# Graph passes gather into a ring of sixteen tiles in place of four; the last pass scatters a block eight steps behind its gather from eight tiles

## What is computed

```python
def gcn_layer(x, src, dst, W, b, n_nodes):              # layer 0, twice
    h = x @ W
    norm = dis[src] * dis[dst]
    agg = segment_sum(h[src] * norm[:, None], dst, n_nodes)
    return agg + h * (dis * dis)[:, None] + b

def _gcn_conv(h, W, b, row, col, norm, num_nodes):      # layer 3, six times
    h = h @ W
    agg = segment_sum(h[row] * norm[:, None], col, num_nodes)
    return agg + b

x = _layernorm(x + layer0(x))     # two GCN convolutions
x = _layernorm(x + layer1(x))     # gated edges
x = _layernorm(x + layer2(x))     # graph attention
x = _layernorm(x + layer3(x))     # GCN widths 128-64-32-16-32-64-128, then h @ Wf + bf
return x
```

## Time and profile before

| what | us |
|---|---|
| three executions: median, lowest, highest | 11700.1, 11695.49, 11714.07 |
| span of the profiled execution, first to last instruction | 11674.7 |
| busy in the span: DVE, POOL, PE, ACT | 8085.7, 7388.3, 6602.9, 5916.2 |
| g1 (689.0 to 1479.9) and g2 (1479.9 to 2402) | 790.9 and 922.1 |
| layers 1 and 2 (2402 to 7066.5) | 4664.5 |
| g3, g4, g5, g6, g7 | 698.5, 608.2, 742.5, 640.3, 646.8 |
| g8 (10402.8 to the end) | 1271.9 |

### The profile page before, as it was taken

One profiled execution on the slowest core, in us unless ns is written; L12 is line 12 of the kernel. 1 busy time (PEld: TensorE's weight loads), 2 busy tenths in 40 slices (PEclk: granted clock), 3 DMA queues, 4 the chain that ended last, 5 costly groups with the idle time before them and its releaser, 6 DMA issues. The chain is left out here.

```text
span 11674.7 us, 142292 instructions
## 1 busy us (share of the span) xinstructions
PE 6602.9 (57%) x32436; PEld 5435.0 (47%) x32436; DVE 8085.7 (69%) x33889; ACT 5916.2 (51%) x13869; POOL 7388.3 (63%) x6801
## 2 busy tenths in 40 slices
PE   5036666656664666677566666753455565543343
PEld 3035655545554666677456565742233343322222
DVE  7357799946667999899888884445466666764444
ACT  0024467757677999899577773321133332322222
POOL 7734478867776888666376664556554555556665
PEclk8568888878886555688678875555577556655555
DMA  4977778832224777444244443433344333332221
GB/s 136 317 236 236 237 270 289 289 96 70 70 70 156 235 234 235 135 141 141 86 154 165 160 165 114 136 105 83 84 131 128 92 97 87 116 88 55 55 57 51
DMA packets 1019502, 1694.48 MB, mean 145 GB/s; under 512 B 304878, under 2 KB 535081, under 8 KB 1018595
## 3 DMA queue, kind: packets, MB, share of 16 engines
q1 hardware_dynamic: 782752, 1361.06, 34.9%
q0 software_dynamic: 175936, 218.82, 8.4%
q10 hardware_dynamic: 59970, 105.49, 2.7%
HBM read 988.03 MB, written 707.78 MB: 145 GB/s over the span
## 5 line engine op out<-in xcount | busy, mean ns | idle before, releaser
L1340 POOL DMA_INDIRECT g_got<-scaled,row_src x2352 | 2230.9, 948 | 1640.0 <-issue 684.0
L298 PE MATMUL g_a_p_z<-sb_L_gnn_W,g_a_u_t 128*128 128x128 f32 (+3 forms) x2574 | 650.8, 397 | 1045.8 <-ACT g_a_u_t L1185 374.3
L902 DVE SCALAR_TENSOR_TENSOR g_sums<-g_got,first,g_sums 128x128 f32<-128x128 f32 (+3 forms) x3136 | 866.0, 276 | 389.4 <-remote 113.4
L298 PEld LDWEIGHTS g_a_p_z<-sb_L_gnn_W,g_a_u_t 128*128 128x128 f32 (+1 forms) x2574 | 482.4, 265 | 1218.4 <-issue 584.0
L906 DVE SCALAR_TENSOR_TENSOR g_sums<-g_sums,cont,g_got 128x128 f32<-128x128 f32 (+3 forms) x3128 | 882.3, 282 | 110.0 <-DVE g_sums L902 74.6
L1185 ACT COPY g_a_u_t<-g_a_p_t 128x512 f32<-128x512 f32 (+3 forms) x495 | 225.3, 455 | 1357.5 <-remote 779.5
L298 PE MATMUL g_bb_p_z<-sb_L_gnn_W,g_bb_u_t 128*128 128x128 f32 (+2 forms) x4302 | 831.4, 361 | 116.5 <-DVE g_bb_z L1077 79.0
L298 PEld LDWEIGHTS g_bb_p_z<-sb_L_gnn_W,g_bb_u_t 128*128 128x128 f32 x4302 | 753.6, 261 | 165.7 <-issue 134.8
L1185 ACT COPY g_bb_u_t<-g_bb_p_t 128x1024 f32<-128x1024 f32 (+2 forms) x294 | 233.8, 795 | 1111.8 <-issue 541.4
L1340 POOL DMA_INDIRECT g_got<-xs,idx_src x392 | 370.8, 946 | 470.1 <-DVE g_a_own L1021 279.1
L1252 POOL DMA_INDIRECT out<-g_a_o,idx_out x396 | 395.4, 998 | 370.3 <-ACT g_a_o L350 254.7
(11 more groups left out here) (495 smaller groups left out, 24005.0 us busy)
## 6 DMA issues: line engine op xcount, KB each, us to landing
raw<-gb_u SPq DMA_DIRECT2D x98, 768.0 KB
xs<-f_o ACTq DMA_DIRECT2D x97, 516.0 KB
f_x<-in_x ACTq DMA_DIRECT2D x97, 512.0 KB
g_bb_own<-in_x SPq DMA_DIRECT2D x97, 512.0 KB
wide<-g_bb_o SPq DMA_DIRECT2D x97, 512.0 KB
g_bb_own<-wide SPq DMA_DIRECT2D x97, 512.0 KB
g_bb_res<-in_x SPq DMA_DIRECT2D x97, 512.0 KB
x<-g_bb_o SPq DMA_DIRECT2D x97, 512.0 KB
```

Source lines behind the costliest of these rows:

```text
L298: last = nc.tensor.matmul(dst_psum[0:p, q * g * width:(q * g + n) * width], turned_tile[0:n * k, q * P:q * P + p], weight[0:n * k, 0:n * w ...
L902: nc.vector.scalar_tensor_tensor(out=self.firsts, in0=new, scalar=first[:, col], in1=self.firsts, op0=ALU.mult, op1=ALU.add).then_inc(run_ ...
L1340: pool.indirect_dma_start(got[b.s4][:, c * row:(c + 1) * row], None, table, bass.IndirectOffsetOnAxis(ap=index[:, b.n * CH + c:b.n * CH + ...
```

## The change

The ring `got` has sixteen tiles, named by block number modulo 16. The gather of block n waits until block n - 16 is combined, and also until the gather of block n - 4 has landed; this second wait is needed because the four landing semaphores stay four. In g1, which also copies a column out of the gathered tile, the wait for that copy moves from n - 4 to n - 16 too. In g8 the output has eight tiles in place of four, the scatter is eight steps behind the gather in place of four, `normalise` waits for the landing of the scatter of block n - 8, and the scatter of block n waits for the landing of that of block n - 4. No arithmetic changes, and the number of DMAs on every engine stays.

```diff
+RING = 16
+OUT_RING = 8
...
-                dve, tile = nc.vector, self.tiles[b.s4 % len(self.tiles)]
+                dve, tile = nc.vector, self.tiles[b.n % len(self.tiles)]
...
-                    if b.after(UNROLL):
-                        nc.scalar.wait_ge(scattered[b.s4], past(scattered[b.s4]) + b.turn * CH * DMA)
+                    if b.after(OUT_RING):
+                        nc.scalar.wait_ge(scattered[b.s4], past(scattered[b.s4]) + (b.turn + 1 - OUT_RING // UNROLL) * CH * DMA)
...
                 nc.gpsimd.wait_ge(self.m_.finished, b.n + 1)
+                if b.after(UNROLL):
+                    nc.gpsimd.wait_ge(scattered[b.s4], past(scattered[b.s4]) + b.turn * CH * DMA)
...
-                        self.o_s[b.s4][:, c * D:(c + 1) * D], None, bounds_check=N - 1, oob_is_err=False
+                        self.o_s[b.n % OUT_RING][:, c * D:(c + 1) * D], None, bounds_check=N - 1, oob_is_err=False
...
-                got = [sb(f"got{s}", [P, CH * row]) for s in range(UNROLL)]
+                got = [sb(f"got{s}", [P, CH * row]) for s in range(RING)]
...
                             if b.after(UNROLL):
-                                pool.wait_ge(mark_a.combined, b.n - UNROLL + 1)
+                                pool.wait_ge(gathered[b.s4], past(gathered[b.s4]) + b.turn * CH * DMA)
+                            if b.after(RING):
+                                pool.wait_ge(mark_a.combined, b.n - RING + 1)
                                 if keep_rows:
-                                    pool.wait_ge(indexed, b.n - UNROLL + 1)
+                                    pool.wait_ge(indexed, b.n - RING + 1)
...
-                            pipeline(pool, [(gather, 0, NBE), (na.scatter, 4, NBA)])
+                            pipeline(pool, [(gather, 0, NBE), (na.scatter, 8, NBA)])
```

More of the change, by code:

```diff
@@ L946, in __init__ @@
                 self.own_s = [sb(f"{n}_own{s}", [P, G * k]) for s in range(2)]
-                self.o_s = [sb(f"{n}_o{s}", [P, G * m]) for s in range(UNROLL if scatters else 2)]
+                self.o_s = [sb(f"{n}_o{s}", [P, G * m]) for s in range(OUT_RING if scatters else 2)]
                 self.from_own = self.deep or self.after or (edges is None and not self.plain)
@@ L1335, in gather @@
                             if b.after(UNROLL):
-                                pool.wait_ge(mark_a.combined, b.n - UNROLL + 1)
+                                pool.wait_ge(gathered[b.s4], past(gathered[b.s4]) + b.turn * CH * DMA)
+                            if b.after(RING):
+                                pool.wait_ge(mark_a.combined, b.n - RING + 1)
                                 if keep_rows:
-                                    pool.wait_ge(indexed, b.n - UNROLL + 1)
+                                    pool.wait_ge(indexed, b.n - RING + 1)
                             for c in range(CH):
                                 pool.indirect_dma_start(
-                                    got[b.s4][:, c * row:(c + 1) * row], None, table,
+                                    got[b.n % RING][:, c * row:(c + 1) * row], None, table,
                                     bass.IndirectOffsetOnAxis(ap=index[:, b.n * CH + c:b.n * CH + c + 1], axis=0)
@@ L1376, in keep_row @@
                             dve.wait_ge(gathered[b.s4], gathers_before(gathered[b.s4], b))
-                            nc.vector.tensor_copy(at_window(row_src, b), got[b.s4][:, k:CH * row:row]
+                            nc.vector.tensor_copy(at_window(row_src, b), got[b.n % RING][:, k:CH * row:row]
                                                   ).then_inc(indexed, 1)
```

## The result

The changed kernel takes 11886.06 us (median of four, 11855.92 to 11898.55) against 11697.8 us before on the same chip: ratio 1.0158, 95% interval 1.0141 to 1.0174, 1.6% slower. 11830 was forecast, range 11620 to 11930. The profiled execution has a span of 11881.7 us and a time of 11883.46.

The account below looks back on a forecast made before the run. The consumer (DVE with PE and ACT), held during POOL's long indirect-DMA runs, sets the pace in most passes; DVE bounds g2. 11674.7 + 128 (six passes +118, g8 +10) + 25.4 gives 11828, said as 11830 us; range 11620 to 11930.

Parts of the forecast that it names:

- the sign of being right: Observation named in advance as confirming the forecast: among others, g3 to g7 each 8 to 30 us longer.
- 12 f: End of g1, g3 to g7: twelve more blocks left when POOL falls silent, each costing f, the busiest engine's 3.16 to 5.57 us.
- 91 - 18.2 T: Start of g1, g3 to g7: first run 91 us longer, sparing 18.2 steady-state blocks of T (6.01 to 7.94 us) each.
- the bound of +189: Upper bound for g1, g3 to g7 in sum, if nothing is combined while POOL issues; +118 us was taken.
- g8: Ring and later scatter in g8: extra steps +30 us, end -21, net taken as +10; bounds -243 and +45.
- The steady state: Middle of g1, g3 to g7: a full ring frees one block per combined block at any size, so no change.
- g2 and the added waits: In g2 POOL can't run ahead: 0, +/-5 us; added landing waits expected to be over when asked.
- The 25.4 us "around the span": Difference between span and median of the kernel before, added to the forecast span 11802.7 to give 11828 us.
- The rule weighed: Skill's rule that only DVE and GpSimd contend, so POOL's runs would not slow PE; forecast doubted it as the whole story.
- rival 1: POOL's runs do no harm: g8 loses its waits, -243, and DVE's waits elsewhere -42 us; 11415 us, chance 0.15.
- 2 (nothing moves): Ring full either way, consumer keeps 9 to 10 us a block in the start run: -20 to +15, 11700 us, chance 0.17.
- 3 (stopped outright): Long run stops the consumer outright, in g8 too: +189 and +45, 11934 us, chance 0.12.

Follow-up runs that it names:

- e5: Ring of sixteen, scatter as before, each gather waiting for the landing of the block just before it; against the kernel before: ratio 1.0213.
- e7: Kernel before plus six stretches of a DVE-PE-ACT chain beside POOL or SP work; a round takes 1.1 us alone, 2.8 when held beside unbroken indirect DMAs.
- e9: Kernel before plus chain stretches with more DVE instructions, a late start, or pauses after 8, 16, 24 DMAs; held from 14.4, 65.5, never, 69, 36 us.
- e10: Kernel before, ring and lag of four, but in g8 each gather waits for the last scatter's landing: ratio 0.9908, g8 1145.9 us.
- e12_after_again: The changed kernel without edit, on another chip, against the kernel before: ratio 1.0261, g8 1255.8 us.
- b: Probe stretch behind the kernel before: engine chain beside 60 unpaused indirect DMAs of 64 values a row; a round takes 1.25 us, then 2.8 from 35.6 us.

## Why the prediction was right, and where it was not

*Direction, place and mechanism: right.* 11830 us was forecast and 11886 measured, a change of +188 us for a forecast +130. The ring makes the loss: in a long first run the consumer is held, and more blocks are left when POOL falls silent. That unbroken runs of indirect DMAs hold the other engines was a reading of coincidences; `e5`, `e7`, `e9` and `e10` show it for these executions. The size by pass was off: 38 to 49 us each in g3 to g7, where the sign of being right was 8 to 30.

*The tail: right.* 12 f was worth 325 us in sum by the forecast and measured 334. By pass it was off both ways: g5 72 and not 55 (72 / 12 = 6.0 us for each block more and not DVE's 4.56), g3 52 and not 62.

*The first run: the term that was mis-sized.* 91 - 18.2 T, the head start less the steady state that it spares, was to give back 207 us in sum and gave 93: in g3 to g7 38 in place of 153. g1 met its number (54.7 for 53), but not by the model's way: its run lasts 94.7 us and not 126, with one interval of 63 us. In g4 the run is 114.8 us and not 126, because a block takes 21 us in it and not the 17 taken from the shorter run in the earlier trace rows; and POOL restarts only 11.6 us after it, for one block alone. When the steady cycle begins at 7979.6, 24 blocks are issued in 136.9 us; before it was 9 in 51.9. So 15 blocks took 85 us where the cycle of before takes 90, a gain of 5, and the forecast had 18. The 241 us of the ring lie even above the bound of +189, which supposed that the cycle follows at once when the run ends; the whole time lies in its range only because g8 came out below its term.

*The steady state: nearly right*, costed at nothing; g4's cycle is 18.1 us in place of 17.7, 7 us in the pass.

*g8: wrong.* +10 was forecast, -46.5 measured in the first trace, and -7 to -9 on the other chips; the program with g8's change alone has the ratio 1.0000. The waits do not go: 187.4 us are left of 254.7. Some 37 of the 46.5 us are how POOL's runs happened to fall in that execution, three steps and not four to a cycle; the same kernel in `e12_after_again` has them as before. What decides between the two stays open, as does why the late scatter without the ring gave 0.9968. The 56 us by which g8 fell below its term hid nearly half of the 123 us that the ring's term missed by. That the sum came nearer than its terms is luck.

*g2 and the added waits: right*, 0 and +2.3 with layers 1 and 2 in it; from g2's first gather to its last it takes 876.8 us, 876.5 before.

*The 25.4 us "around the span": wrong in kind.* The changed kernel's time is 1.8 us above its own span. The 25.4 is, by that, mostly that the profiled execution of before was a quick one, so it was right to add it to reach the median and wrong to name it what lies before and behind.

*The rule weighed.* The Trainium skill, SBUF — State Buffer, "Who interferes with whom", says that "PE and ACT never wait on anyone". In `e7_probe` ACT starts 1.75 us after the matmul that it waits for, with no longer instruction anywhere. As a rule of the memory ports this may stand, since DVE's copy beside POOL's copies was the longer one (0.48 us in place of 0.23) and ACT's stayed at 0.27. As a reason to expect that POOL's indirect DMAs can't delay PE and ACT it does not, and rival 1 fell with it.

*Rivals.* 1 (waits go, faster) is refuted in this kernel by g8's waits and in `e7`; but its number, g8 near 1030 us, shows the right place: with short pauses g8 came to 1146. 2 (nothing moves) fell with intervals of 21 us. 3 (stopped outright) overrates the hold in g4 and g5, where a block still passes every 21 us, but is near the truth in g1 and g3 with their 63 and 50 us; in g8, where it had +45, it was wrong. Its 11934 us were only 48 above the result.

*Open.* The ratio is 1.0158 on one chip and 1.0261 on the other. g8 explains 37 us of this, 0.3%, and the six passes agree within 11 us in the traces (+241 and +252); but the traced execution of `e12_after_again` is 50 us below its median, and the rest isn't explained. What it is that fills was not found either. One rival stands: each execution timed here was recorded, with its spans and clocks, so it may be the writing of that record that makes the others wait beside indirect DMAs, and the runs can't tell whether the hold is there in an unrecorded execution. The mere number of instructions recorded is not it: in the stretch at 3675 us above they are 13 a us and the packets of transfers 116 a us, where b has 3 and 26.

## What to carry to other kernels

Look at how long POOL issues indirect DMAs without a pause. If the consumers' hand-overs get longer late in such runs and recover only after them, more buffers make it worse; a wait for the last landing after some eight DMAs costs POOL 1.5 to 1.8 us and may give back more: 119 us in g8 here. It isn't free: a pause after every four cost 218 us in the six passes, and one after every eight 36 us in g3. And a deeper ring ahead of a consumer that sets the pace gained nothing in the middle here and left more blocks for the end.

## What was not expected of the hardware

- Hand-overs between DVE, PE and ACT went from 1.1 us a round to 2.8 after 36 us of unbroken indirect DMAs, with all instructions as long as before, and held some 8 us beyond their end. In a denser stretch it began after 14.4 us and a round took 7.0. In both nearly every held round is a multiple of 0.70 us: 2.1, 2.8, 3.5, 6.3, 7.0, 7.7.
- The size of the gathered rows made no difference (64 or 16 values: onset 35.6 us in both); direct loads from SP had no effect.
- Pauses of 1.7 us after every eight indirect DMAs kept the chain free for the 75 us that it lasts; after every sixteen it was held after 69 us, after every 24 after 36 us.
- The same kernel ran g8 in two ways, in 1225 us with cycles of mostly three steps and in 1256 with cycles of four.
- DVE's copy 128x128 took 0.38 us beside indirect DMAs in the part that is not held, 0.48 beside POOL copies, and 0.23 alone.
